# First attention block: scores computed once, key-major, with the row maxima added by matmuls; the stacked operands gathered by DMA

## What is computed

```python
B, D, T = x.shape                      # 16, 128, 256;  NH = 8 heads, dk = 16
q = jnp.transpose(x, (0, 2, 1)) @ Wq.T
qh = q.reshape(B, T, NH, dk).transpose(0, 2, 1, 3)
scores = scale * jnp.einsum('bhqd,bhkd->bhqk', qh, qh)
logits = (scores * cmask + (1.0 - cmask) * NEG) * rmask     # key mask, query mask
attn = jax.nn.softmax(logits, axis=-1)
ctx = jnp.einsum('bhqk,bhkd->bhqd', attn, qh)
out = ctx.transpose(0, 2, 1, 3).reshape(B, T, D) @ Wo.T     # added to x after a transpose
```

## Time and profile before

| | us |
|---|---|
| median of 3 runs | 860.46 |
| lowest, highest | 860.18, 918.24 |
| span of the profiled execution | 859.8 |
| V copy of group 0 to V copy of group 7 (36.83, 198.31) | 161.5 |
| last exponential of the first block ends | 217.0 |
| attention's first matmul starts | 234.2 |

### The profile page before, as it was taken

The page is one execution under the profiler, slowest core; times in us unless marked ns, Lnnn a source line. Parts: engine busy times, 40 slices in busy tenths (PEclk is TensorE's granted clock), DMA queues, the critical chain, the costliest instruction groups (busy, mean ns, idle before and its releaser), DMA issues. The chain is left out here.

```text
span 859.8 us, 13910 instructions
## 1 busy us (share of the span) xinstructions
PE 807.7 (94%) x5156; PEld 651.0 (76%) x5156; DVE 441.8 (51%) x807; ACT 455.9 (53%) x1164; POOL 198.9 (23%) x176
## 2 busy tenths in 40 slices
PE   5899999998599999999999999999999999889997
PEld 3655555554388888888888888888888888767775
DVE  1687788776334443444545444545444335445443
ACT  2376667676344553554464455464454365475553
POOL 3276666663101111110111111111011032200000
PEclk9999999998599999999999999999999999999999
DMA  7312122220200000000000000000000001020001
GB/s 206 75 61 69 55 73 73 73 62 26 84 27 1 1 1 2 1 1 2 1 1 1 1 0 0 0 0 0 1 1 1 1 26 38 25 98 25 1 24 49
DMA packets 27242, 25.47 MB, mean 30 GB/s; under 512 B 10160, under 2 KB 23872, under 8 KB 27200
## 3 DMA queue, kind: packets, MB, share of 16 engines
q1 hardware_dynamic: 27200, 24.90, 9.8%
HBM read 20.70 MB, written 4.19 MB: 29 GB/s over the span
## 5 line engine op out<-in xcount | busy, mean ns | idle before, releaser
L890 ACT ACTIVATE probs<-bank,nm 128x128 f32<-128x128 f32 x256 | 90.5, 366 | 221.0 <-DVE nm L972 221.0
L1028 POOL TENSOR_TENSOR probs<-probs,rinv 128x512 f32<-128x512 f32 x64 | 66.6, 1041 | 433.7 <-DVE rinv L981 433.7
L645 PE MATMUL bank<-x1h,w_hi 128*128 128x512 f32 x256 | 112.8, 441 | 5.0 <-DVE x1l L958 5.0
L645 PE MATMUL bank<-x1h,w_lo 128*128 128x512 f32 x256 | 102.1, 399 | 0.0
L645 PE MATMUL bank<-x1l,w_hi 128*128 128x512 f32 x256 | 102.0, 398 | 0.0
L513 ACT ACTIVATE pt<-ring 128x1024 f32<-128x1024 f32 x64 | 65.8, 1029 | 54.2 <-PE ring L396 52.5
L1002 DVE COPY Vv<-bank 128x512 f32<-128x512 f32 x64 | 44.3, 692 | 82.2 <-PE bank L645 82.2
L593 DVE TENSOR_REDUCE mcol<-ring 128x4 fp32r<-128x1024 f32 x64 | 77.9, 1218 | 6.8 <-PE ring L385 6.7
L645 PE MATMUL bank<-w_hi,x1h 128*128 128x256 f32 x256 | 71.9, 281 | 0.0
L962 DVE COPY pT<-ring 128x512 f32<-128x512 f32 x64 | 44.2, 690 | 53.8 <-PE ring L770 53.6
L645 PE MATMUL bank<-w_hi,x1l 128*128 128x256 f32 x256 | 71.7, 280 | 0.0
(11 more groups left out here) (160 smaller groups left out, 1746.5 us busy)
## 6 DMA issues: line engine op xcount, KB each, us to landing
stage<-in_L_cond_qkv_w_dram SPq DMA_DIRECT2D x12, 512.0 KB, 4.5
mb<-in_cond_dram SPq DMA_DIRECT2D x8, 256.0 KB, 3.9
xs<-in_x_dram SPq DMA_DIRECT2D x8, 256.0 KB, 4.3
stage<-in_L_cond_out_w_dram SPq DMA_DIRECT2D x4, 512.0 KB, 3.5
kept<-X SPq DMA_DIRECT2D x1, 2048.0 KB, 8.0
raw<-in_L_cond_ffn_w_dram SPq DMA_DIRECT2D x8, 256.0 KB, 2.8
xk<-kept SPq DMA_DIRECT2D x1, 2048.0 KB, 8.3
out_dram<-X SPq DMA_DIRECT2D x4, 512.0 KB, 2.9
```

The costliest lines, as they stand in the source:

```text
L645: last = nc.tensor.matmul(bank, w(k), x(k), start=(start and i == 0), stop=(stop and i == len(terms) - 1))
L890: last = nc.scalar.activation(probs[:, h % 2, b, :], Sb[:, b * T:(b + 1) * T], ACT.Exp, bias=nm[:, h % 2, b:b + 1], accum_out=sums[:, h % ...
L1028: pool.tensor_tensor(probs[:, h % 2, :, :], probs[:, h % 2, :, :], rinv[:, h % 2, :, None].to_broadcast([P, GB, T]), ALU.mult).then_inc(po ...
```

## The change

In the first block:

- **Operands.** POOL multiplies x with the mask before the projection and splits the product (`masked`, four instructions a group). PE projects once per group with split weights (`project`, three fp32r matmuls of 512 columns); ACT rounds the result to `qh`, DVE forms `ql`. SP writes qh three times and ql once to a DRAM buffer `qd` (`gather`), and reads them back stacked, 48 partitions by 4 units by 512 at partitions 0 and at 64, for `QS` and for `KS` (`spread`), plus four one-row DMAs for the mask rows (`rows`). The per-unit projection, `hs`, `qst`, `kst`, R and C are gone.
- **Scores.** They are computed once, key-major, four matmuls for half a unit, into two banks (`scores`). DVE takes maxima of 512 elements at a time, a bank at a time, into a column per 128 of `mx`: by symmetry the maxima over the queries of a key are those over the keys of a query. PE adds them to the same banks by eight matmuls a unit with a broadcast column of `mx` as weights and the identity as moving operand (`shift`). ACT takes the exponentials 512 at a time. All four banks of `ring` now hold unshifted and then shifted scores, so the next scores of a half wait for its exponentials.
- `pv` is cut in two parts by key tile; both need all four exponentials of the unit. The sums of a group leave in halves. X is read for V directly; `xs` is gone.
- The biases are loaded as 5 row-wise DMAs and transposed by one matmul; before, they were gathered element by element. The loops are written out (36 + 1 steps).
- The first block splits 12 chunks; the 4 chunks of `out_w` are loaded in the attention stage in 8 pieces of 256 KB, rounded by ACT and POOL at the ends of its first 8 steps, into `wo_hi` and `wo_lo`; PE waits for `pool_wo` before it uses a piece. The later weights of `ffn` are loaded after them.

The diff, cut to its core:

```diff
+                def rows(g):
+                    sp.wait_ge(pool_x, g + 1)
+                    if g >= 2:
+                        sp.wait_ge(pe_s, 16 * (g - 1))
+                    for dst, row in ((QS, mb), (KS, nb)):
+                        for s in range(2):
+                            r = 64 * s + ROWS_ONE
+                            sp.dma_start(dst[r:r + 1, g % 2, :, :].bitcast(F32),
+                                         row[0:1, g % 2, None, :].to_broadcast([1, 4, 512])).then_inc(l_q[g % 2], 16)
+                def gather(g):
+                    q = qd[g % 2]
+                    sp.wait_ge(act_q1, g + 1)
+                    for c in (0, 1, 3):
+                        sp.dma_start(q[:, c], qh[:, :].bitcast(F32)).then_inc(l_qd[g % 2], 16)
+                    sp.wait_ge(dve_ql, g + 1)
+                    sp.dma_start(q[:, 2], ql[:, :].bitcast(F32)).then_inc(l_qd[g % 2], 16)
+                def spread(g):
+                    v = qd[g % 2].rearrange("(j s) c d n -> s (c d) j n", s=2)
+                    sp.wait_ge(l_qd[g % 2], 64 * (g // 2 + 1))
+                    for dst, c in ((KS, 1), (QS, 0)):
+                        for s in range(2):
+                            sp.dma_start(dst[64 * s:64 * s + 3 * DK, g % 2, :, :].bitcast(F32),
+                                         v[s, DK * c:DK * (c + 3)]).then_inc(l_q[g % 2], 16)
...
+                for g in range(NGR - 1):
+                    rows(g + 1)
+                    gather(g + 1)
+                    if g + 2 < NGR:
+                        mask(g + 2)
+                    spread(g + 1)
+                    for c in (2 * g + 2, 2 * g + 3):
+                        if c < CHUNKS:
+                            weights(c)
...
+                def scores(n, b):
+                    g, j = divmod(n, 4)
+                    if j == 0 and b == 0:
+                        pe.wait_ge(l_q[g % 2], LQ * (g // 2 + 1))
+                    wait(pe, act_exp, 4 * (n - 1) + 2 * b + 2)
+                    for kt in range(2):
+                        for s in range(2):
...
+                            last = nc.tensor.matmul(ring[:, 2 * b + s, kt * 256:kt * 256 + 256],
+                                                    KS[r, g % 2, j, k0:k0 + P], QS[r, g % 2, j, b * 256:b * 256 + 256],
+                                                    start=(kt == 0), stop=True, skip_group_check=True)
+                def shift(n, b):
+                    for s in range(2):
+                        wait(pe, dve_max, 4 * n + 2 * b + s + 1)
+                        for qt in range(2):
...
+                            last = nc.tensor.matmul(out, mx[:, 2 * b + s, qt:qt + 1].to_broadcast([P, P]),
+                                                    identr[:, None, :].to_broadcast([P, 2, P]),
+                                                    start=False, stop=True, skip_group_check=True)
...
+                for n in range(LAST + 1):
+                    if n < UNITS:
+                        scores(n, 0)
+                    if n == 0:
+                        modulations(2)
+                    if 0 <= n - 1 < UNITS:
+                        shift(n - 1, 1)
...
+                    if n % 4 == 1 and n // 4 + 1 < NGR:
+                        project(n // 4 + 1)
+                    if n % 4 == 3 and n // 4 + 1 < NGR:
+                        values(n // 4 + 1)
+                    if 0 <= n - 1 < UNITS:
...
+                        wait(pe, act_exp, 4 * n)
+                        pv(n - 1, 0)
+                    if n < UNITS:
+                        shift(n, 0)
+                        scores(n, 1)
+                    if n == 0:
+                        modulations(3)
+                    if 0 <= n - 1 < UNITS:
+                        pv(n - 1, 1)
```

More of the change, by code:

```diff
@@ new lines, in _ @@
+                sp.dma_start(X[:, 4:B, :], x[4:B].rearrange("b p d -> p b d")).then_inc(l_x, 16)
+                rows(0)
+                gather(0)
+                spread(0)
+                weights(0)
+                weights(1)
+                for g in range(NGR - 1):
[7 more added lines that the diff above has]
+                            weights(c)
@@ L378, in scores @@
-                def scores(u, ju, b):
-                    wait(pe, dve_max, 2 * u + b)
-                    for qt in range(2):
-                        for s in range(2):
-                            r = slice(64 * s, 64 * s + 64)
-                            q0 = b * 256 + qt * P
-                            last = nc.tensor.matmul(ring[:, s, qt * 256:qt * 256 + 256], qst[r, ju, q0:q0 + P],
-                                                    kst[r, ju, b * 256:b * 256 + 256], start=True, stop=True)
-                    last.then_inc(pe_s, 1)
@@ L389, in shifted @@
-                def shifted(u, ju, b):
-                    wait(pe, act_exp, 2 * u + b)
-                    for kt in range(2):
-                        for s in range(2):
-                            r = slice(64 * s, 64 * s + 64)
-                            k0 = b * 256 + kt * P
-                            last = nc.tensor.matmul(ring[:, 2 + s, kt * 256:kt * 256 + 256], kst[r, ju, k0:k0 + P],
-                                                    qst2[r, b * 256:b * 256 + 256], start=True, stop=True)
-                    last.then_inc(pe_st, 1)
@@ L661, in hidden, with attention @@
                     lambda k: x2[1][:, k, bass.ds(gn * GT, GT)], True, True, range(KT))
-def attention(nc, sem, sb, kept, saved, norm1, dve_n1, pe_n1, norm2, X, w_hi, w_lo, ada, gb1, qkvb, qb_s, ident,
-              banks, ffn_w1, ffn_w2, x2f, act_x2, dve_x2, pe_f1):
+def attention(nc, sem, sb, kept, saved, norm1, dve_n1, pe_n1, norm2, X, w_hi, w_lo, wo_hi, wo_lo, ada, gb1, qkvb,
+              qb_s, ident, banks, out_w, ffn_w1, ffn_w2, x2f, act_x2, dve_x2, pe_f1):
     UN = NG * H
@@ L1039, in _, with ffn @@
                 run(pool, step)
-def ffn(nc, sem, sb, kept, norm2, x2f, act_x2, dve_x2, pe_f1, X, w_hi, w_lo, ada, gb2, b1, ident, banks, out):
+def ffn(nc, sem, sb, kept, norm2, x2f, act_x2, dve_x2, pe_f1, X, w_hi, w_lo, wo_hi, wo_lo, ada, gb2, b1, ident, banks,
+        out):
     UN = NG * MC
```

645 lines of the change are left out of this document (312 added, 333 removed).

## The result

| | median us | lowest to highest | profiled span us | mean granted clock |
|---|---|---|---|---|
| before | 862.13 (4 runs) | 860.18 to 918.24 | 859.8 | 0.981 |
| after | 920.69 (4 runs) | 917.04 to 922.16 | 920.0 | 0.937 |

The change makes the kernel slower by 6.9%: the ratio of after to before is 1.0693, with an interval of [1.0657, 1.0729]. One run of before, the 918.24, was a disturbed one and is left out of the ratio; the other three lie between 860.18 and 863.81. The forecast was 870 with a range of 826 to 892, so the result lies above the range.

A forecast was written before the change was run, and what follows sets the result against it. PE bounds the kernel, but a DMA chain 4.5 us longer than its cover, plus a cold step, makes groups 24.8 us against 23.4. That adds 11, the end takes off 1.5: span 869.3, median 870, range 826 to 892.

The forecast's parts named there:

- What bounds, and where it waits: First block: PE leads; after the change it waits once per group, 3 to 6 us, for the DMA into QS or KS.
- The sign of the chain's excess: Projection, gather and spread before a group's first scores: 18.4 us, 4.5 us longer than the three steps meant to cover them.
- the rate of the transfers in the DMA chain: Gather and spread at 218 GB/s with a first landing of 1.9 us: gather 6.4 us, spread 8.8, waits 0.2.
- Both ends of my bounds: DMA chain: 14.4 us at the bulk rate of 337 GB/s, 27 us with transfers one after the other.
- The price of a us of chain: First block: each us of the gather and spread chain beyond 18.4 costs 7 us of the whole.
- The cold step: First step behind each group's DMA wait: PE at 1.2 GHz, adding 2.1 us, 6.4 instead of 4.3.
- The warm steps of PE, DVE and ACT: First block, full clock: steps of 4.2 us, two per group of 4.85; a warm group 18.2 us against 23.4.
- The start: Before the attention groups: gather lands near 19.8, spread near 28.5; unit 1's first exponential at 42.4 against 41.28.
- Rival 3: Spread slower than 218 GB/s, same wait at a group's first scores; with a chain of 22 us, 895 us; chance 0.15.
- The end: After the first block's last exponential: half of the sums leave earlier, -1.5 us.
- The moved weight loads: Attention: the `out_w` pieces cost nothing beside half-idle ACT and POOL; 1 to 2 us once if the first piece's cover failed.
- Rival 1: First block: transfers run at the bulk rate and the clock stays high, groups of 18.2 us, about 820; chance 0.13.

## Why the prediction was wrong, and where it was right

- **What bounds, and where it waits: right.** PE waits once per group, at the first scores, for the DMA into `QS`, and V copies, scores and exponentials queue behind it. The sign of the chain's excess was right, its size not.
- **The step that failed: the rate of the transfers in the DMA chain.** Gather 6.4 forecast, 9.0 measured. Spread with its waits 9.0 forecast, 12.1 measured. Both ends of my bounds held the values (chain 14.4 and 27 by the earlier trace rows, measured 24.3), and I took a value from the middle and then let the range end at a chain of about 22. The step put gather and spread at 218 GB/s with 1.9 us around the bytes. The 218 GB/s came from the slope between a 64 KB and a 256 KB load of 128 partitions: that row knows nothing of how many engines a gather of eight rows gets, nor of half the partitions. That the Trainium skill has the same number for half of the partitions made me trust it for both transfers. For the gather it was no bound at all: half of the engines at half of the 337 GB/s of the earlier trace rows is 168, which makes 1.9 + 6.2 = 8.1 us, and I had the reason in the text and did not carry it into the sum. The runs put in its place: gather 167 to 187 GB/s with half the engines; spread 175, below the 225 of a half, and 2.5 to 3.2 us around the bytes (on average 11.6 less 1.57 MB at 175 is 2.6; 8.4 less 2.10 MB at 403 with the spread of 128 is 3.2) where the same reckoning of my 9.0 gives 1.8. The Trainium skill's port table, in the section that I cited for the half, would have given 218 x 48/64 = 164, an estimate from the Trainium skill's figure, and I did not count the 48 rows against it.
- **The price of a us of chain: right.** Rival 3 had this mechanism and 7 us of the whole for each us of the chain. 5.9 us more chain are 41; its 895 had assumed a chain of 22. On average a group was 6.15 us longer than forecast, 5.7 by the chain and the rest by its first step (6.9 against 6.4). I had put 0.15 on it; bounds from 14.4 to 27 gave no right to 0.42 for a band of 2 us.
- **The cold step: right.** 6.4 forecast, 6.8 measured, 6.5 against 4.4 in one and the same kernel.
- **The warm steps of PE, DVE and ACT: right.** The three other steps, up to the next wait, take 14.5 us in the group shown where I had 13.9; a group without stall 18.8 where I had 18.2, at 1.00 of the clock.
- **The start: mis-sized by the same term.** First scores at 35.4 instead of 28.5: the spread issued at 23.98 instead of 19.8, then 11.5 us instead of 8.8. I had also counted 4.8 us for the first gather (15 to 19.8) where the chain had 6.4; it took 10.3. Moving X won 2.0 of it.
- **The end: a small miss.** From the last exponential (277.14) to the attention's first projection (294.17) it is 17.0 us against 17.2 before: the 1.5 us that I took off are 0.2.
- **The moved weight loads: right.** No wait of PE for `wo_hi` or `wo_lo` stands in the attention, and from the last exponential to the end it is 642.9 us after and 642.8 before.
- **The sum.** Start 6.9, the first group 5.1 (24.5 from unit 1 to unit 4, forecast 19.4), six groups 36.9 (30.95 - 24.8 each), the last units 0.3, the end 1.3: 50.5 us, and 869.3 + 50.5 = 919.8 against a span of 920.0.
- **Rival 1 (820), with the chain really hidden.** The gather a group ahead gives 838.7: 10.4 us later at unit 1, 3.1 more to unit 4, 3.2 in six groups, 0.6 and 1.3 behind: 18.6 together. (The 48.6 for unit 4 in that rival is a slip: its own terms, 34.6 + 14.4 + 1, give 50.0.) The arithmetic of the change is worth 4.6 us a group (23.4 to 18.8); its transfers, in its order of work, cost 12.1 (18.8 to 30.95), of which 2.1 to 2.4 are the cold step.

## What to carry to other kernels

When work is moved from an engine to a DMA, the first question is not how many bytes but how many DMA engines and which partitions each transfer can reach; with no row of such a shape, the slow bound is the one to plan with, and the range has to reach it. Look at DMA share and GB/s together: here a low share with a low rate was a shape that left engines idle, and a full share with a low rate was a target that they did not reach fast. And a chain that is longer than its cover is cheaper to start one turn earlier than to speed up: with both transfers mended in place the kernel, its mask rows left out, took 867 us beside 861 of before, with neither mended but the gather a group ahead it was 2.6% faster than before.

## What the runs showed of the hardware

- Transfers over 48 partitions of one half ran at 169 to 187 GB/s (mean of a group's spread), over 64 of one half at 222 to 230, over 32 at 223 to 234, over all 128 at 394 to 409, all with the DMA engines busy throughout and with 2 KB pieces from the same buffer. I had not expected 48 to be slower than 32.
- Queued transfers to the lower and the upper 64 partitions did not reach the rate of one transfer over both: 12.4 us against 8.4 for the same bytes, on average.
- A DMA to DRAM whose slowest dimension is 8 kept the engines 0.51 busy at 167 to 184 GB/s, with 16 it was 0.99 to 1.00 and 325 to 333.
- In one kernel, at the same place of the loop, the granted clock was 0.50 at the end of a wait of PE of 3.25 us and 1.00 at the end of one of 2.84; the step behind took 6.54 us and 4.41.
